# Local attention layers on one core: masks in the scores' row tiles, and a new order of the stages on all engines

## The chip, the cores and the metric

The program runs on one core of one Trainium2 chip. The metric is the device time of one execution in microseconds. Three executions took 3747.89, 3753.0 and 3758.61 us; the median is 3753.0 us.

## The reference

Inputs are x and a context of shape (32, 128, 128): 32 batch elements, 128 tokens, width 128. The model is a gated cross-attention, a stack of six local-attention layers with an MLP each, a second gated cross-attention and an int8 product. The change is in the six local layers:

```
for i in range(DEPTH):                                   # 6
    x = attn_layer(shift_tokens(x), Wqkv[i], ...) + x    # 16 heads of 64, window 32
    x = ffn_layer(shift_tokens(x), ...) + x              # layer norm, 128 -> 2 x 341, a * gelu(gate), -> 128
...
    q = l2norm(q) * qs;  k = l2norm(k) * ksc             # then rotary tables on both
    mask = (it < jb) | (it > jb + w) | (jb == -1)        # a window sees itself and the window before
    sim = where(mask, -max, einsum(q, k) * QK_SCALE)     # (windows of 32 queries) x (64 keys)
    attn = softmax(sim, -1)
    out = einsum(attn, v)                                # then out @ Wo
```

## The kernel before

**Units and groups.** A unit is one batch element in one layer: 6 x 32 = 192 units. A group is four units (512 tokens), and the output projection, the MLP and its layer norm run once a group. Everything is fp32, except the masks, which are bf16.

**The software pipeline.** Each engine (TensorE `pe`, ScalarE `act`, VectorE `dve`, GpSimd `pool`, and SyncE `sp` for the DMAs) has a loop over steps at the end of its function in `local_layers`. In step s it calls its stages for unit s, s-1, s-2 and so on, in the order in which they are written there. No scheduler moves anything: each engine works through its own list in order, and semaphores hold a stage until what it reads is made and what it overwrites is read. The number in `scores(step - 2)` is the lag of that stage.

**A unit's way.** `project` makes q, k and v (lines L697; two products of 512 columns each). q and k share one pair of PSUM banks, QK_PAIR: ScalarE squares what stands there (`square`, L874), VectorE multiplies it with the cosine and sine tables (`products`, L1012 and L1013), and only then is the pair free for the next projection. VectorE sums the squares (L1020) and clamps them (L1028), ScalarE makes the reciprocal norms (L883, L885), GpSimd adds the rotary halves (`rotate`, L1121) and multiplies with the norms (`normalise`, L1129). TensorE turns q and k (`transpose_qk`, L707), ScalarE copies them out (L892). `scores` first writes the masks into the scores' banks (L717, a product of the identity with the mask table) and adds the products of q and k (L726), in array tiles of 64 rows and 32 columns. VectorE takes the maxima and subtracts them (L1033, L1041), ScalarE exponentiates (L899), VectorE sums rows (L1049, L1051), GpSimd normalises (L1113), TensorE turns the weights (L738), ScalarE copies them (L906), and TensorE mixes the values (`mix`, L763) in tiles of 64x64. ScalarE copies the mix (L913). v goes through ScalarE's copy (L867) and four DMAs that place it again in other partitions (`place_v`).

**Once a group.** `project_out` (L777), the mean (L786), the variance (L794), three upper products of the MLP in tiles of 128, 128 and 85 hidden channels (`mlp_up`, L804), their GELU on ScalarE (`mlp_gelu`, L965) and product on VectorE (`mlp_hidden`, L1075), and `mlp_down` (L815). The steps repeat with period four: one step has no group work, one has the mean and the MLP products, one the variance, one the output projection.

**PSUM.** Pair 0 of banks is the scores', pair 1 is QK_PAIR. All other stages take pairs 2 and 3 in turn, in the order of the table ALTERNATING, which follows TensorE's order. A stage therefore waits until the stage two places before it has been read out.

Of the kernel before, what the change touches and what calls it, by code (L numbers as in the profile page):

```python
# [47 lines left out]
CONSTS = 2 * P + NEAR + 4 * HD + 4  # L48
# [62 lines left out]
def build(nc, dram):  # L111
    stack = ExitStack()
    with stack:
# [14 lines left out]
        tables = consts[:, 2 * P + NEAR:CONSTS - 4].rearrange("p (k s d) -> p k s d", k=4, s=2)  # L128
        ident_bf = sb("ident_bf", [P, P], BF16)
        mask_band = sb("mask_band", [P, IT, NEAR], BF16)  # L130
        mask_past = sb("mask_past", [P, GB, P], BF16)
# [8 lines left out]
        MASKS = 2 + GB  # L140
# [404 lines left out]
        def local_layers(phase):  # L545
            here = ExitStack()
            with here:
# [37 lines left out]
                for n in ("squared", "producted", "summed", "rotations", "normalised", "turned", "copied"))  # L585
# [14 lines left out]
            ALTERNATING = (("mix", 4, 1), ("v", 2, 1), ("up0", 10, GB), ("mean", 6, GB), ("up1", 10, GB), ("variance", 7, GB),  # L600
                           ("up2", 10, GB), ("probs", 3, 1), ("out", 4, GB), ("k", 1, 1), ("down", 10, GB), ("q", 1, 1))
# [76 lines left out]
            def pe(pe):  # L678
# [33 lines left out]
                def scores(u):  # L712
# [97 lines left out]
                def mlp_down(g):  # L810
# [3 lines left out]
                    for t, (o, n) in enumerate(FTILES):  # L814
                        mm = pe.matmul(pairs[i][:, 0:GT], w_2[0:n, t, :], gelu[0:n, t, :], start=t == 0,  # L815
                                       stop=t == len(FTILES) - 1)
                    mm.then_inc(down_made, 1)

                for step in range(UNITS + LAST):
                    project(step, 0)  # L820
                    mix(step - 4)
                    project(step - 2, 2)
                    mlp_up(step - 10, 0)
                    scores(step - 2)
                    project(step, 1)
                    mlp_mean(step - 6)
                    mlp_up(step - 10, 1)
                    mlp_variance(step - 7)
                    mlp_up(step - 10, 2)
                    transpose_probs(step - 3)  # L830
                    project_out(step - 4)
                    transpose_qk(step - 1, 1)
                    mlp_down(step - 10)
                    transpose_qk(step - 1, 0)
                phase_end(pe)

            def act(act):
# [121 lines left out]
                def mlp_gelu(g, t):  # L959
                    o, n = FTILES[t]  # L960
                    tables_at["exp"] = False
                    act.wait_ge(up_made, 3 * g + t + 1)
# [5 lines left out]
                for step in range(-1, UNITS + LAST):  # L968
                    square(step, 0)
                    prepare(step + 1)  # L970
                    mlp_affine(step - 10)
                    mlp_root(step - 8)
                    mlp_square(step - 7)
                    copy_mix(step - 4)
                    reciprocal_norms(step - 1)
                    mlp_shift(step - 5)
                    mlp_gelu(step - 10, 0)
                    copy_v(step - 2)
                    square(step, 1)
                    mlp_log(step - 7)  # L980
                    mlp_gelu(step - 10, 1)
                    mlp_gelu(step - 10, 2)
                    copy_probs(step - 3)
                    copy_qk(step - 1, 1)
                    exponentials(step - 2)
                    copy_qk(step - 1, 0)
                phase_end(act)

            def dve(dve):
# [82 lines left out]
                def mlp_hidden(g, t):  # L1072
                    o, n = FTILES[t]
                    dve.wait_ge(gelu_made, 3 * g + t + 1)
# [11 lines left out]
                for step in range(UNITS + LAST):  # L1086
                    if step < UNITS and step % NB == 0:
                        start_layer(step // NB)
                    row_sums(step - 3)
                    products(step, 0)  # L1090
# [3 lines left out]
                    mlp_hidden(step - 10, 1)  # L1094
# [772 lines left out]
```

## Time and profile before

| | |
|---|---|
| median of three executions | 3753.0 us |
| profiled execution | 3750.37 us |
| its span, first to last instruction | 3748.6 us |
| granted TensorE clock, mean | 0.985 |
| TensorE busy | 3555.1 us, 95% |
| VectorE busy | 2719.1 us, 73% |
| ScalarE busy | 2447.7 us, 65% |
| GpSimd busy | 2283.3 us, 61% |

Busy time counts matmuls with modelled ends, which overlap; where the text needs the cost of a stage, it is the distance from its first start to the next stage's first start. An fp32 matmul stands in the trace as two records. In rows of a timeline the last bracket is the idle time before the row and what ended it.

### The profile page before, as it was taken

To read this page: it belongs to the slowest core of one execution; us is meant where nothing else is said; L and a number is where in the kernel's file an instruction comes from. 1 tells how busy PE (TensorE), PEld (TensorE's weight loads), DVE (VectorE), ACT (ScalarE), POOL (GpSimd) and SP (SyncE) were. 2 spreads that over 40 slices of the span, in tenths; PEclk is the share of its full clock that TensorE was granted. 3 is DMA by queue.
4 is the path that set the end of the run, shared out by engine and by line. 5 is a ranking of instruction groups with operands and counts; after the bars stand their busy time and mean duration, and the time that the engine had idled before them with its cause. 6 is when DMAs were issued, how large, how long until landed. Compare 5 with 4: busy or idle time off the path is not lost.

```text
span 3748.6 us, 131464 instructions
## 1 busy us (share of the span) xinstructions
PE 3555.1 (95%) x57538; PEld 2099.7 (56%) x57538; DVE 2719.1 (73%) x3104; ACT 2447.7 (65%) x4388; POOL 2283.3 (61%) x1216
## 2 busy tenths in 40 slices
PE   8979999999999999999999999999999999997996
PEld 4535555555555555555555555555555555553554
DVE  6858777777777777777777777777777777763787
ACT  6856666666666666666666666666666666664985
POOL 1227666666666666666666666666666666652666
PEclk9989999999999999999999999999999999998998
DMA  2001111111111111111111111111112111120000
GB/s 86 2 1 42 36 36 32 46 47 42 36 31 36 53 40 38 36 36 47 45 40 36 35 32 53 42 41 36 30 37 58 32 40 36 36 58 2 2 10 15
DMA packets 90943, 134.71 MB, mean 36 GB/s; under 512 B 23686, under 2 KB 37380, under 8 KB 89988
## 3 DMA queue, kind: packets, MB, share of 16 engines
q1 hardware_dynamic: 90372, 126.29, 13.0%
q8 instruction: 456, 7.47, 0.9%
q14 instruction: 115, 0.94, 0.1%
HBM read 23.48 MB, written 2.10 MB: 7 GB/s over the span
## 4 chain that ended last, share of the span: by engine, by line
PE 81%; ACT 6%; DVE 6%; issue 5%; POOL 1%; DMA 0%; SPq 0%; POOLq 0%; DVEq 0%; ACTq 0%
PE psum L697 29%; PE psum L777 8%; PE psum L763 8%; PE psum L726 7%; PE psum L804 7%; PE psum L707 6%; PE psum L815 3%; PE psum L738 2%; PE psum L717 2%; DVE f_times_sin L1013 2%; ACT f_squares L874 2%; ACT f_probsT L906 1%; ACT x_expo L1446 1%; PE psum L786 1%; PE psum L794 1%
## 5 line engine op out<-in xcount | busy, mean ns | idle before, releaser
L1121 POOL TENSOR_TENSOR f_rotated<-f_times_cos,f_times_sin 128x1024 f32<-128x1024 f32 x384 | 906.4, 2361 | 527.3 <-DVE f_times_sin L1013 527.3
L697 PE MATMUL psum<-w_qkv,f_xs 128*128 128x512 f32 x2304 | 1135.7, 616 | 40.2 <-DVE f_times_sin L1013 35.4
L874 ACT ACTIVATE f_squares<-psum 128x1024 f32<-128x1024 f32 x384 | 393.8, 1026 | 530.1 <-PE psum L697 530.1
L1129 POOL TENSOR_TENSOR f_rotated<-f_rotated,f_rnorm 128x1024 f32<-128x1024 f32 x384 | 722.3, 1902 | 26.5 <-ACT f_rnorm L885 26.5
L1113 POOL TENSOR_TENSOR f_probs<-f_probs,f_rowsum 128x1024 f32<-128x1024 f32 x192 | 365.2, 1902 | 537.6 <-DVE f_rowsum L1051 537.6
L892 ACT COPY f_qkT<-psum 128x1024 f32<-128x1024 f32 x384 | 388.4, 1011 | 351.5 <-PE psum L707 346.6
L697 PEld LDWEIGHTS psum<-w_qkv,f_xs 128*128 128x128 f32 x2304 | 393.7, 191 | 362.0 <-issue 284.6
L1012 DVE TENSOR_TENSOR f_times_cos<-psum,rot 128x1024 f32<-128x1024 f32 x384 | 460.4, 1199 | 88.7 <-ACT f_squares L874 86.5
L1013 DVE TENSOR_TENSOR f_times_sin<-psum,rot 128x1024 f32<-128x1024 f32 x384 | 465.6, 1212 | 0.0
L1020 DVE TENSOR_REDUCE f_sumsq<-f_squares 128x16 f32<-128x1024 f32 x384 | 451.8, 1208 | 0.0
L707 PE MATMUL psum<-consts,f_rotated 128*128 128x128 f32 x3072 | 408.1, 278 | 44.8 <-DVE f_gelu L1075 27.7
L707 PEld LDWEIGHTS psum<-consts,f_rotated 128*128 128x128 f32 x3072 | 340.1, 141 | 145.1 <-issue 50.5
L1033 DVE TENSOR_REDUCE f_negmax<-psum 128x16 f32<-128x1024 f32 x192 | 234.8, 1223 | 217.9 <-PE psum L726 217.7
L763 PEld LDWEIGHTS psum<-f_probsT,f_v 64*64 64x64 f32 x6144 | 262.1, 135 | 145.8 <-issue 145.5
L777 PE MATMUL psum<-f_outT,w_o 128*128 128x512 f32 x768 | 339.1, 595 | 1.2 <-ACT f_outT L913 1.2
L763 PE MATMUL psum<-f_probsT,f_v 64*64 64x64 f32 (+1 forms) x6144 | 309.3, 228 | 1.3 <-issue 1.1
L763 PE MATMUL psum<-f_probsT,f_v_moved 64*64 64x32 f32 (+1 forms) x12288 | 306.7, 217 | 0.0
L726 PEld LDWEIGHTS psum<-f_qkT 64*32 64x32 f32 x24576 | 250.1, 105 | 82.9 <-issue 82.8
L763 PEld LDWEIGHTS psum<-f_probsT,f_v_moved 64*64 64x64 f32 x12288 | 285.4, 135 | 0.0
L726 PE MATMUL psum<-f_qkT 64*32 64x64 f32 (+1 forms) x24576 | 281.7, 219 | 1.0 <-issue 1.0
L804 PE MATMUL psum<-f_xn,w 128*128 128x512 f32 (+1 forms) x576 | 265.9, 598 | 7.4 <-ACT f_xn L955 6.7
L738 PEld LDWEIGHTS psum<-consts,f_probs 128*128 128x128 f32 x1536 | 175.9, 141 | 111.2 <-issue 78.4
(179 smaller groups left out, 5237.3 us busy)
## 6 DMA issues: line engine op xcount, KB each, us to landing
f_v_moved<-f_v SPq DMA_DIRECT2D x768, 128.0 KB, 2.5
w_qkv<-in_l_wqkv SPq DMA_DIRECT2D x18, 512.0 KB, 3.7
w_o<-in_l_wo SPq DMA_DIRECT2D x6, 512.0 KB, 4.4
w_qkv<-in_ctxT SPq DMA_DIRECT2D x1, 2048.0 KB, 8.3
out<-x_f_result SPq DMA_DIRECT2D x8, 256.0 KB, 2.2
w<-in_l_w SPq DMA_DIRECT2D x6, 341.0 KB
xres<-in_xT SPq DMA_DIRECT2D x1, 1536.0 KB, 8.8
x_ctx<-in_ctxT SPq DMA_DIRECT2D x1, 1536.0 KB, 12.0
```

What stands on the lines that cost most here:

```text
L697: mm = pe.matmul(pairs[i][:, j * BANK:(j + 1) * BANK], xs[g % 2][:, u % GB, :], w_qkv[:, part * INNER + j * BANK:part * INNER + (j + 1) * ...
L707: tr = pe.transpose(pairs[i][:, t * S:(t + 1) * S], rotated[u % 2][:, part, 2 * t:2 * t + 2, :].rearrange("p h d -> p (h d)"), ident)
L726: mm = pe.matmul(pairs[SCORE_PAIR][these, at:at + near.stop - near.start], qkT[u % 2][rows, 0, t, these], qkT[u % 2][rows, 1, t, near], st ...
L763: mm = pe.matmul(pairs[i][cols, at + queries.start:at + queries.stop], values, probsT[u % 2][rows, j, queries], start=True, stop=True, til ...
L777: mm = pe.matmul(pairs[i][:, 0:GT], w_o[:, t, :], outT[:, t, :], start=t == 0, stop=t == IT - 1)
L804: mm = pe.matmul(pairs[i][0:n, a * BANK:a * BANK + GT], w_1[:, a * FF + o:a * FF + o + n], xn[:, :], start=True, stop=True)
L874: act.activation(squares[part][:, :], pairs[QK_PAIR], ACT.Square).then_inc(squared[part], 1)
L1012: dve.tensor_tensor(halves(times_cos[part][:, :]), halves(pair), table(0), ALU.mult)
L1013: dve.tensor_tensor(halves(times_sin[part][:, :]), halves(pair)[:, ::-1], table(1), ALU.mult).then_inc(producted[part], 1)
L1020: dve.tensor_reduce(sumsq[u % 2][:, part * H:(part + 1) * H], squares[part][:, :].rearrange("p (s h d) -> p h s d", s=2, h=H), axis=XY, op ...
L1121: pool.tensor_tensor(rotated[u % 2][:, part].rearrange("p h (s d) -> p s h d", s=2), halves(times_cos[part][:, :]), halves(times_sin[part] ...
L1129: pool.tensor_tensor(rt, rt, rnorm[u % 2][:, part * H:(part + 1) * H].unsqueeze(2).broadcast_to([P, H, HD]), ALU.mult).then_inc(normalised ...
```

## The change

Two things change, and both are in the local layers.

**Masks.** Before, each of the two mask products multiplies a 128x128 identity with the mask table for all 128 query rows. Now the table holds the 64 kinds of query rows that differ (the first window's 32, and the later windows' 32), twice, once for each half of the partitions, and a new matrix `mask_pick` picks for each of the 128 queries its kind. So a mask product contracts over 64 rows, and the two products, one for each bank, stand in the upper and the lower 64 rows of the array. `mask_pick` is one more block of 128 columns in the constants and one more copy to bf16 on VectorE at the start.

**Order.** The stages stand in another order on TensorE, ScalarE, VectorE and GpSimd; v is projected one unit after q and k rather than two; the three upper products are made in the order 2, 1, 0; some stages that ended a step on one engine now begin the next one with a lag one higher (the sum of squares of k, the clamp), and some group stages of ScalarE and GpSimd move to another lag.

```
-                        pe.matmul(pairs[SCORE_PAIR][:, j * BANK:(j + 1) * BANK], ident_bf[:, :],
-                                  mask_band[:, :, :].rearrange("p g n -> p (g n)"), start=True, stop=False)
+                        rows = slice(HD * j, HD * j + HD)
+                        pe.matmul(pairs[SCORE_PAIR][:, j * BANK:(j + 1) * BANK], mask_pick[rows, :],
+                                  mask_band[rows, :, :].rearrange("p g n -> p (g n)"), start=True, stop=False,
+                                  tile_position=(rows.start, 0))
...
-                    banks.fill(pe, i, (hidden_made, 3 * g + t + 1))
+                    banks.fill(pe, i, (hidden_made, 3 * (g + 1) - t))
...
                 for step in range(UNITS + LAST):          # TensorE
+                    mlp_up(step - 10, 2)
                     project(step, 0)
+                    mlp_up(step - 10, 1)
+                    mlp_up(step - 10, 0)
+                    project(step - 1, 2)
+                    scores(step - 2)
                     mix(step - 4)
-                    project(step - 2, 2)
-                    mlp_up(step - 10, 0)
-                    scores(step - 2)
+                    mlp_mean(step - 6)
                     project(step, 1)
-                    mlp_mean(step - 6)
-                    mlp_up(step - 10, 1)
                     mlp_variance(step - 7)
-                    mlp_up(step - 10, 2)
                     transpose_probs(step - 3)
                     project_out(step - 4)
-                    transpose_qk(step - 1, 1)
                     mlp_down(step - 10)
                     transpose_qk(step - 1, 0)
+                    transpose_qk(step - 1, 1)
...
+                for step in range(-2, UNITS + LAST):      # ScalarE, whole
+                    mlp_gelu(step - 10, 2)
+                    mlp_shift(step - 6)
+                    mlp_gelu(step - 10, 1)
                     square(step, 0)
+                    mlp_affine(step - 9)
+                    mlp_gelu(step - 10, 0)
+                    copy_v(step - 1)
+                    reciprocal_norms(step - 1)
                     mlp_root(step - 8)
+                    prepare(step + 2)
                     mlp_square(step - 7)
                     copy_mix(step - 4)
                     square(step, 1)
                     mlp_log(step - 7)
                     copy_probs(step - 3)
+                    copy_qk(step - 1, 0)
+                    exponentials(step - 2)
                     copy_qk(step - 1, 1)
-                    exponentials(step - 2)
-                    copy_qk(step - 1, 0)
...
                     products(step, 0)                     # VectorE, in part
-                    mlp_hidden(step - 10, 0)
+                    sum_squares(step, 0)
+                    row_maxima(step - 2)
                     mlp_centre(step - 6)
-                    row_maxima(step - 2)
...
-                    sum_squares(step, 1)
-                    clamp_norms(step)
...
                     normalise_probs(step - 3)             # GpSimd, whole
+                    normalise(step - 1, 0)
                     normalise(step - 1, 1)
-                    normalise(step - 1, 0)
                     rotate(step, 0)
                     rotate(step, 1)
+                    mlp_scale(step - 8)
```

On TensorE, before, around a step with the mean and the MLP products. L697 is a projection, L738 turns the weights, L707 turns q and k, L804 are the upper products, L815 the down product:

```order
6410 L697 MATMUL psum<-w_qkv,f_xs 128x512 x2
6411 L786 MATMUL psum<-f_mlp_xs,mean_mat 128x512
6412 L804 MATMUL psum<-f_xn,w 128x512 x2
6413 L804 MATMUL psum<-f_xn,w 85x512 x2
6414 L738 MATMUL psum<-consts,f_probs 128x128 x8
6415 L707 MATMUL psum<-consts,f_rotated 128x128 x8
6416 L815 MATMUL psum<-f_gelu,w 128x512 x3
6417 L707 MATMUL psum<-consts,f_rotated 128x128 x8
```

The same engine in the change, from the k projection of the step without group work to the masks of the step with the MLP products (L698, L741, L708, L807 and L719 are L697, L738, L707, L804 and L717 of before):

```order
6221 L698 MATMUL psum<-w_qkv,f_xs 128x512 x2
6222 L741 MATMUL psum<-consts,f_probs 128x128 x8
6223 L708 MATMUL psum<-consts,f_rotated 128x128 x16
6224 L807 MATMUL psum<-f_xn,w 85x512 x2
6225 L698 MATMUL psum<-w_qkv,f_xs 128x512 x2
6226 L807 MATMUL psum<-f_xn,w 128x512 x4
6227 L698 MATMUL psum<-w_qkv,f_xs 128x512 x2
6228 L719 MATMUL psum<-mask_band,mask_pick 128x512 x2
```

All three upper products have moved ahead of the masks, the first of them to between the turn of k and the next q projection; before, two stood right ahead of the turns and one behind the value projection. And later in that step, in the change, ending with the first projections of the next step:

```order
6277 L789 MATMUL psum<-f_mlp_xs,mean_mat 128x512
6278 L698 MATMUL psum<-w_qkv,f_xs 128x512 x2
6279 L741 MATMUL psum<-consts,f_probs 128x128 x8
6280 L818 MATMUL psum<-f_gelu,w 128x512 x3
6281 L708 MATMUL psum<-consts,f_rotated 128x128 x16
6282 L698 MATMUL psum<-w_qkv,f_xs 128x512 x4
```

The down product now stands ahead of both turns, and the q and the v projection stand together (x4). The mix rows, which stood between them, follow the scores.

## Rows read from the trace of the kernel before

**Rows 1.** The page, part 1: busy us (share of the span) x instructions, by engine.
```profile
PE 3555.1 (95%) x57538; PEld 2099.7 (56%) x57538; DVE 2719.1 (73%) x3104; ACT 2447.7 (65%) x4388; POOL 2283.3 (61%) x1216
```
**Rows 2.** Timeline of TensorE (start, length, operation, [idle before]), the output projections.
```profile
996.04 4.46 PE L777 MATMUL psum<-f_outT,w_o 128*128 128x512 f32 x10
...
1061.10 7.03 PE L777 MATMUL psum<-f_outT,w_o 128*128 128x512 f32 x16
```
**Rows 3.** Timeline of TensorE, step without group work, to the next mix.
```profile
1009.95 0.59 PE L717 MATMUL psum<-mask_band,ident_bf 128*128 128x512 bf16 x2
1010.48 1.46 PE L726 MATMUL psum<-f_qkT 64*32 64x32 f32 x128
1011.87 1.98 PE L697 MATMUL psum<-w_qkv,f_xs 128*128 128x512 f32 x4
1013.69 1.04 PE L738 MATMUL psum<-consts,f_probs 128*128 128x128 f32 x8
1014.56 1.04 PE L707 MATMUL psum<-consts,f_rotated 128*128 128x128 f32 x8
1015.87 1.09 PE L707 MATMUL psum<-consts,f_rotated 128*128 128x128 f32 x8 [0.27 <-ACT f_probsT L906]
1017.36 1.98 PE L697 MATMUL psum<-w_qkv,f_xs 128*128 128x512 f32 x4 [0.39 <-DVE f_times_sin L1013]
1019.27 0.27 PE L763 MATMUL psum<-f_probsT,f_v 64*64 64x64 f32 x1
```
**Rows 4.** Timeline of TensorE, from the mean to the down product.
```profile
1028.08 1.02 PE L786 MATMUL psum<-f_mlp_xs,mean_mat 128*128 128x512 f32 x2
1028.94 3.60 PE L804 MATMUL psum<-f_xn,w 128*128 128x512 f32 x8
1032.38 1.09 PE L738 MATMUL psum<-consts,f_probs 128*128 128x128 f32 x8
1034.09 1.10 PE L707 MATMUL psum<-consts,f_rotated 128*128 128x128 f32 x8 [0.62 <-DVE f_gelu L1075]
1035.03 2.74 PE L815 MATMUL psum<-f_gelu,w 128*128 128x512 f32 x6
```
**Rows 5.** Timeline of TensorE in the second cross-attention, from 128*128 to 128*32 tiles.
```profile
3500.62 1.02 PE L1290 MATMUL psum<-y,x_wq 128*128 128x512 f32 x2
3501.58 1.08 PE L1327 MATMUL psum<-x_probsT,x_vpad 128*32 128x128 f32 x32
```
**Rows 6.** Timeline of TensorE in the first cross-attention: masks behind 32*128 tiles.
```profile
66.21 0.61 PE L294 MATMUL psum<-mask_past,ident_bf 128*128 128x512 bf16 x2
66.75 1.16 PE L301 MATMUL psum<-x_queries,x_keys 32*128 32x128 f32 x16
```
**Rows 7.** Timeline of TensorE in the second cross-attention: two 32-row tiles.
```profile
3472.13 1.13 PE L1303 MATMUL psum<-x_keys,x_queries 32*128 32x512 f32 x4
3473.19 0.98 PE L1313 MATMUL psum<-consts,x_expo 128*128 128x128 f32 x7
```
**Rows 8.** Timelines of ScalarE and VectorE around the stages of rows 3 and 4.
```profile
1013.89 1.02 ACT L874 ACTIVATE f_squares<-psum 128x1024 f32<-128x1024 f32 x1 [2.05 <-PE psum L697]
1014.81 1.01 ACT L906 COPY f_probsT<-psum 128x1024 f32<-128x1024 f32 x1
1015.70 1.03 ACT L892 COPY f_qkT<-psum 128x1024 f32<-128x1024 f32 x1
...
1022.42 1.28 ACT L965 ACT_TABLE_LOAD   x1
1024.54 0.69 ACT L965 ACTIVATE f_gelu<-psum,b 128x512 f32<-128x512 f32 x1 [0.84 <-PE psum L804]
...
1016.09 1.21 DVE L1013 TENSOR_TENSOR f_times_sin<-psum,rot 128x1024 f32<-128x1024 f32 x1
...
1025.26 0.75 DVE L1075 SCALAR_TENSOR_TENSOR f_gelu<-psum,b,f_gelu 128x512 f32<-128x512 f32 x1 [1.78 <-ACT f_gelu L965]
```
**Rows 9.** Timeline of GpSimd, the two products with the norms.
```profile
1009.75 3.77 POOL L1129 TENSOR_TENSOR f_rotated<-f_rotated,f_rnorm 128x1024 f32<-128x1024 f32 x2
```

More of the change, by code:

```diff
@@ L47 @@
 HALFV = INNER // 2
-CONSTS = 2 * P + NEAR + 4 * HD + 4
+CONSTS = 3 * P + NEAR + 4 * HD + 4
 VSTEP = P + XD
@@ L139, in build @@
         phase_over = sem("phase_over")
-        MASKS = 2 + GB
+        MASKS = 3 + GB
         def group(t, g):
@@ L599, in local_layers @@
             LAST = 11
-            ALTERNATING = (("mix", 4, 1), ("v", 2, 1), ("up0", 10, GB), ("mean", 6, GB), ("up1", 10, GB), ("variance", 7, GB),
-                           ("up2", 10, GB), ("probs", 3, 1), ("out", 4, GB), ("k", 1, 1), ("down", 10, GB), ("q", 1, 1))
+            ALTERNATING = (("up2", 10, GB), ("up1", 10, GB), ("up0", 10, GB), ("v", 1, 1), ("mix", 4, 1), ("mean", 6, GB),
+                           ("variance", 7, GB), ("probs", 3, 1), ("out", 4, GB), ("down", 10, GB), ("q", 1, 1), ("k", 1, 1))
             pair_of, turn = {}, 0
@@ L813, in mlp_down @@
                     pe.wait_ge(hidden_made, 3 * g + 3)
-                    for t, (o, n) in enumerate(FTILES):
-                        mm = pe.matmul(pairs[i][:, 0:GT], w_2[0:n, t, :], gelu[0:n, t, :], start=t == 0,
-                                       stop=t == len(FTILES) - 1)
+                    for t, (o, n) in reversed(list(enumerate(FTILES))):
+                        mm = pe.matmul(pairs[i][:, 0:GT], w_2[0:n, t, :], gelu[0:n, t, :], start=t == len(FTILES) - 1,
+                                       stop=t == 0)
                     mm.then_inc(down_made, 1)
                 for step in range(UNITS + LAST):
+                    mlp_up(step - 10, 2)
                     project(step, 0)
+                    mlp_up(step - 10, 1)
+                    mlp_up(step - 10, 0)
+                    project(step - 1, 2)
+                    scores(step - 2)
                     mix(step - 4)
-                    project(step - 2, 2)
-                    mlp_up(step - 10, 0)
-                    scores(step - 2)
+                    mlp_mean(step - 6)
                     project(step, 1)
-                    mlp_mean(step - 6)
-                    mlp_up(step - 10, 1)
                     mlp_variance(step - 7)
-                    mlp_up(step - 10, 2)
                     transpose_probs(step - 3)
                     project_out(step - 4)
-                    transpose_qk(step - 1, 1)
                     mlp_down(step - 10)
                     transpose_qk(step - 1, 0)
+                    transpose_qk(step - 1, 1)
                 phase_end(pe)
@@ L1088, in dve @@
                         start_layer(step // NB)
+                    sum_squares(step - 1, 1)
+                    clamp_norms(step - 1)
                     row_sums(step - 3)
+                    mlp_hidden(step - 10, 2)
+                    mlp_hidden(step - 10, 1)
+                    mlp_hidden(step - 10, 0)
                     products(step, 0)
-                    mlp_hidden(step - 10, 0)
+                    sum_squares(step, 0)
+                    row_maxima(step - 2)
                     mlp_centre(step - 6)
-                    row_maxima(step - 2)
-                    mlp_hidden(step - 10, 1)
-                    mlp_hidden(step - 10, 2)
                     lower(step - 2)
@@ L1098, in dve @@
                     add_out(step - 4)
-                    sum_squares(step, 0)
                     add_down(step - 10)
-                    sum_squares(step, 1)
-                    clamp_norms(step)
                 phase_end(dve)
@@ L1807, in shape_constants @@
     parts = (np.arange(P)[:, None] % XPAD // XD == np.arange(4)[None, :])
-    return np.concatenate([np.eye(P), band, past] + both + [parts], axis=1).astype(np.float32)
+    kinds = np.concatenate([band[0:2 * WIN]] * 2)
+    row = np.arange(P)
+    kind = np.where(row < WIN, row, WIN + row % WIN)
+    pick = np.arange(P)[:, None] % (2 * WIN) == kind[None, :]
+    return np.concatenate([np.eye(P), kinds, past, pick] + both + [parts], axis=1).astype(np.float32)
 def halves_first(w):
```

18 lines of the change are left out of this document (5 added, 13 removed).

## The prediction

> **What bounds the kernel now.** The page comes first: TensorE is busy 95% of the span [rows 1]. So TensorE's own stream sets the time, and a change is worth what it takes out of that stream: work, changes of tile size, or waits. The local layers repeat every four units. In TensorE's timeline the output projection L777 starts at 996.04 and again at 1061.10 us [rows 2]: a group of four units takes 65.06 us. There are 48 groups (6 layers of 32 elements), some 3,120 of the 3,750 us.
>
> The timeline in order of time then shows where the 65.06 us go. The number to read is the distance from one row's start to the next one's, since a row's own length includes the pipeline's tail. In a step without group work [rows 3]: masks 0.53, scores 1.39, k projection L697 1.82, turn of the weights 0.87, turn of q, a pause, turn of k, a pause, next q projection. I read three pauses off the starts:
>
> - The turn of k starts 1.31 after the turn of q (1014.56 to 1015.87) where eight transposes need 0.87: 0.44 lost. The row names the copy of the turned weights on ScalarE.
> - Eight transposes after a wait take 0.94 (1034.09 to 1035.03, [rows 4]), so k's end at 1016.80; the q projection starts at 1017.36: 0.56 lost, and the row names VectorE's product with the sine table, which reads the PSUM pair that q and k share. The q projection then takes 1.91 to the mix where 1.72 of work (twice the 0.86 of two matmul records, 1028.08 to 1028.94) and 0.09 for the change of tile size make 1.81: 0.10 more, a weight load that a waiting engine could not fetch early.
> - In the step with the MLP's upper products [rows 4], the turn of q starts 1.71 after the turn of the weights: 0.84 lost, named to VectorE's L1075 on f_gelu, which frees the PSUM pair that the third upper product used; and 0.07 more for the first load.
>
> **The change part by part, on TensorE.** All sums are per unit (192) or per group (48).
>
> Masks. Masks to scores, 0.53, holds two bf16 products over all 128 rows (2 x 0.22) and 0.09 for the change from the full array to the scores' tiles. What a change of size costs is also seen where only the columns change: L1290 (two records, full array) to L1327 (128*32) is 0.96, and two such records without a change are 0.86 (L786 to L804), so 0.10. The two new products sit in different halves of the rows and write different banks. Nearest row: L1303, two 32-row tiles with 512 columns, writing two banks. Four records in 1.06 [rows 7]; one after another four fp32 records are 1.72, side by side two passes are 0.86 plus the change 0.09 and an open first load 0.10 = 1.05. So pairs in different row tiles run together, and I take 0.22 for both masks instead of 0.43: -0.21 a unit. Bound from the other side: not together, 0.
>
> First loads. After a change back to the full array, the first fp32 matmul is 0.10 late (k's projection 1.82 [rows 3] against 1.72; the value projection stands behind small tiles as well, so twice a unit). Afterwards the value projection stands right behind q or the upper products, in the same layout: 1.72. -0.10 a unit. In its place the masks now come right after a change. What a bf16 load costs there: L294 follows 32-row tiles and takes 0.54 to its successor [rows 6], L717 without such a change 0.53 [rows 3]: 0.01. The Trainium skill ("TensorE: Matmul & The Clock Gate", The mechanism and LDWEIGHTS) says that a load overlaps running matmuls only in another row group and takes columns / 1.2 GHz, an estimated 0.107 here; by that the masks' load lies open and the total is 18 us higher. The row of this case has 0.01, and I go by it.
>
> Changes of tile size. Before, four a unit: into the mix, out, into the scores, out. Afterwards also four: into 64x128, to 64x32, to 64x64, out. No row shows a change between two small sizes with the same 64 rows. Bounds: 0, or the 0.09 that every recorded change costs. The nearest row is L1290 to L1327, where the rows stay 128 and only the columns change, at the full 0.10 [rows 5]. So I take 0.09 and no gain; the other end is 2 x 0.09 x 192 = 35 us less. The Trainium skill ("TensorEngine Tiling (Array Packing)", Key Properties) says that a change of the tiling mode drains the array while a change of tile doesn't. That rule speaks against a gain from putting scores and mix together; read loosely, with 64 rows as one mode, it would give the 35 us. The column row agrees with the strict reading.
>
> Waits. I walked the new order on all four engines with durations from the rows. Take the k projection's start in a plain step as 0 (before: 1011.87).
> ScalarE squares k at 2.02, copies the turned weights at 2.94 to 3.95, and k's turn can start at 4.00 [rows 3, 8]. This chain is untouched: 0.44 stays.
> K's turn ends at 4.93. VectorE's sine product starts at 4.22, takes 1.21 [rows 8] and lets a q projection start at 5.49. Before, q stood there and waited. Now the first upper product (85 columns wide, 1.72) does: it needs the pair of the turned q, which ScalarE now copies first, 3.83 to 4.86, free at 4.90. So it starts at 4.93, and q at 6.65, without a wait: -0.56 and its reload -0.10.
> The other upper products run at 8.37 and 10.09, the value projection at 11.80. It needs the pair of the second upper product: done at 10.26 (8.37 + 1.72 + the 0.17 by which a record outlasts the next start), GELU 0.69, VectorE's product 0.75, free near 11.80 [rows 8]. No wait, but only just. ScalarE's table load of 1.28 falls at about 6.7, ahead of the first GELU and hidden behind the q projection.
> The last upper product's VectorE step is done near 13.5, the down product asks for it at about 20: the wait of 0.84 and its 0.07 are gone. The down product now stands ahead of both turns, and k's turn then waits for VectorE to add it into y; I find 0.10, with 0.06 of reload.
> The waits in the steps with the variance and the output projection have unchanged chains and cancel. Together: -0.66 -0.91 +0.16 = -1.41 a group.
>
> Other engines. VectorE gets one copy of 128x128 at the start, beside the loads: 0.2 us at most. The constants are 64 KB longer in one load. Neither counts. The sum of squares of k and the clamp move behind the next step's start, so the normalisation of a unit starts later: in my walk GpSimd is done with k's 7.8 us into the step that turns it, and TensorE comes for it at 9.4; before the same pair of 1.9 us multiplications was done at 1013.52 for turns that started at 1014.56 [rows 3, 9].
>
> **Sum.** 4 x (-0.21 - 0.10) - 1.41 = -2.65 a group, 62.4 instead of 65.06. Over 47.5 groups (the first ones are not full): -126 us. The profiled execution took 3750.4 us (span 3748.6), so 3624; the median of the runs is 2.6 above it: 3627.
>
> **The rivals.**
> 1. Changes between the small sizes are free, or the mix's first loads hide behind the scores: 35 us more, 3592. For it: the row halves stay the same. Against: the column row.
> 2. The masks don't run side by side in 64x128 tiles (+0.21 x 192 = 40), or their first load lies open like an fp32 one (+0.10 x 192 = 19): 3646 to 3667. For it: no 64*128 row exists. Against: L1303.
> 3. The waits only move. The walk has two places with under 0.05 us to spare (the upper product after the copy of q, the value projection after the second VectorE product). If both steps lose all again, only masks and loads are left: 60 us, 3693. For it: every engine is in order, and ScalarE's table load sits in that step. Against: a late copy by 0.2 costs 0.2 a group, 10 us, not all.
> 4. Slower: normalisation. GpSimd's two products of 1.9 us start when ScalarE has made the norms; ScalarE now does that behind the copy of v, and VectorE's part behind the next step's start. To spare: 1.5 us. If the norms come later than that, TensorE waits before the turn of k in every unit, and from 1.5 + 126/192 = 2.2 us late the gain is used up. Two more VectorE operations of 1.2 us in that chain make 2.4: (2.4 - 2.2) x 192 = 38 us over before, 3791. I find no such pair in the order, and the products of the next q stand behind the clamp.
> 5. No effect, TensorE's stream held by something that the trace hides: 3750.
>
> **How the numbers follow.** Forecast 62% (own range 3608 to 3645: the walk's small margins, 10 us each way, and the masks' load), rival 1 15%, rival 2 10%, rival 3 7%, rival 4 4%, rival 5 2%. The range 3590 to 3672 holds the first three. 0.3% is 11 us, about what a measurement tells from no change; faster by more than that are the first four, 94%.
>
> **What would show it.** In the new timeline: masks to scores 0.32 (right) or 0.53 (rival 2); scores to mix about 1.39 with the first mix row 0.09 late (rival 1: 1.30); value projection 1.72; first upper product right behind k's turn, q after it without an idle remark; no idle of 0.6 named to L1075 before a turn; groups of 62.4. A row of the turn waiting for GpSimd's f_rotated would mean rival 4. The forecast fails if the period of the groups is above 63.2 or below 61.8.

## The result and the profile after

The change made the kernel slower: 3938.7 us (median of four executions) against 3752.4 before, ratio 1.050, 95% interval 1.047 to 1.053. The forecast was 3627, faster.

The page of the changed kernel, part 1 (busy us, share, instructions), and its chain by engine:

```profile
span 3939.5 us, 131465 instructions
...
PE 3587.2 (91%) x57538; PEld 2138.5 (54%) x57538; DVE 2838.7 (72%) x3105; ACT 2444.7 (62%) x4388; POOL 2284.6 (58%) x1216
...
PE 80%; issue 10%; ACT 5%; DVE 3%; POOL 1%; DMA 0%; SPq 0%; POOLq 0%; DVEq 0%; ACTq 0%
```

In the chain of before, "issue" had 5%.

Read this against [rows 1]. The instructions of TensorE are the same in number, and no other engine is near its limit. But TensorE is idle for 3939.5 - 3587.2 = 352 us where it was 3748.6 - 3555.1 = 194. Its busy time grew by 32 us too, and the mean granted clock fell from 0.985 to 0.971.

What the forecast said of single places is there, but for one. TensorE's timeline of the changed kernel, from the turn of k in the step with the upper products to the mix (the window's edge cuts the first row; rows of one or two instructions within the mix are left out):

```profile
1548.74 0.82 PE L708 MATMUL psum<-consts,f_rotated 128*128 128x128 f32 x6
1549.39 1.93 PE L807 MATMUL psum<-f_xn,w 128*85 128x512 f32 x4
1551.17 1.88 PE L698 MATMUL psum<-w_qkv,f_xs 128*128 128x512 f32 x4
1552.88 3.60 PE L807 MATMUL psum<-f_xn,w 128*128 128x512 f32 x8
1556.33 1.98 PE L698 MATMUL psum<-w_qkv,f_xs 128*128 128x512 f32 x4
1558.24 0.39 PE L719 MATMUL psum<-mask_band,mask_pick 64*128 64x512 bf16 x2
1558.56 1.46 PE L729 MATMUL psum<-f_qkT 64*32 64x32 f32 x128
1559.95 0.27 PE L766 MATMUL psum<-f_probsT,f_v 64*64 64x64 f32 x1
...
1562.62 0.21 PE L766 MATMUL psum<-f_probsT,f_v_moved 64*64 64x64 f32 x1 [1.30 <-issue]
```

Masks to scores 0.32, scores to mix 1.39, the first upper product right behind the turn of k, then q 1.78 later with no idle remark: as written. The value projection is the exception. It was to take 1.72 and takes 1.91 (1556.33 to 1558.24): 0.10 is the change to the masks' tiles, and 0.10 an open first load, because that load has to wait for VectorE to free the PSUM pair, once a group (PEld are the weight loads):

```profile
PEld psum L698 <- DVE f_gelu L1078: 30.4, 45, 0.7
```

The last line of the timeline is the new thing. In the middle of the mix TensorE stands still for 1.30 us, and the row names no engine, no semaphore and no DMA, only "issue": it waited for nothing that the profile shows. TensorE's waits, of before and then of after (whom it waited for: us in total, times, longest):

```profile
PE psum L697 <- DVE f_times_sin L1013: 35.4, 57, 3.5
PE psum L707 <- DVE f_gelu L1075: 27.7, 45, 0.6
PE psum L707 <- ACT f_probsT L906: 13.6, 50, 0.3
...
PE psum L763 <- issue: 1.1, 1, 1.1
```

```profile
PE psum L766 <- issue: 188.4, 124, 2.7
PE psum L729 <- issue: 19.8, 34, 1.0
...
PE psum L708 <- ACT f_probsT L909: 13.3, 50, 0.3
PE psum L698 <- DVE f_times_sin L1016: 12.3, 10, 3.5
```

The two waits that the forecast wanted gone are gone (35.4 to 12.3; the one on f_gelu ahead of a turn has no row any more), and the third stayed as said. In their place stand 208 us of pauses inside the blocks of mix and scores.

**Where they fall.** TensorE's timeline of the changed kernel around one unit in which the scores and the projection behind the mix are hit (most rows of the mix are left out):

```profile
1539.20 1.15 PE L729 MATMUL psum<-f_qkT 64*32 64x32 f32 x98
1541.16 0.45 PE L729 MATMUL psum<-f_qkT 64*32 64x32 f32 x30 [0.81 <-issue]
...
1541.67 0.35 PE L766 MATMUL psum<-f_probsT,f_v_moved 64*64 64x64 f32 x10
...
1543.07 0.70 PE L698 MATMUL psum<-w_qkv,f_xs 128*128 128x512 f32 x1
1545.00 1.45 PE L698 MATMUL psum<-w_qkv,f_xs 128*128 128x512 f32 x3 [1.23 <-issue]
```

Count the instructions from one pause to the next: 30 products of scores, 96 of the mix and 1 of the projection, each with its weight load, and the load of the next. That is 255, and a wait for a semaphore in between is an instruction too. The DMA part of the page has a queue for instructions:

```profile
q8 instruction: 456, 7.47, 0.8%
```

456 packets with 7.47 MB, 16 KB each. TensorE's 57,538 matmuls, 57,538 loads, 1,656 waits for semaphores and 4 drains are 116,736 instructions, which is 456 x 256 exactly: one packet of this queue is 256 instructions of TensorE. Number them in the order of the trace, and 157 of the 158 pauses in scores and mix (207 us) lie at the same place modulo 256, within two instructions; without the waits for semaphores in the count they scatter over all places.

The trace also has the time of every packet, and it ties the two together. The pause at the k-th of these borders ends 1.1 to 1.6 us after the end of the k-th packet, in all 157 cases, and in no run here is a border crossed earlier than 1.08 us after the end of its packet. A packet takes 0.9 to 1.9 us, and the nearest two in any run start 3.20 us apart.

In before the queue moved the same 456 packets, and TensorE had two such pauses, of 0.5 us each, in the scores (its one idle remark in a mix, 1.1 us, stands once in every run, at another place modulo 256). What changed is how fast the instructions are used up: the 256 of a block of scores take 1.39 us and the 192 of a mix 1.53, and now they stand back to back, 448 instructions in 2.9 us, where before a value projection (16 instructions in 1.82) stood between them [rows 3].

**The clock.** Mean values of the changed kernel in four stretches (us from the start: length, busy us and instructions of each engine, then the granted clock of TensorE, the DMA share, GB/s), and its timeline there:

```profile
1430.00:1434.00 4.00, 4.00 (x74) 1.82 (x76) 3.21 (x5) 3.31 (x4) 1.95 (x2) 1.00 0.00 0
1434.00:1438.10 4.10, 2.43 (x181) 2.23 (x165) 4.07 (x4) 2.33 (x6) 3.61 (x3) 0.99 0.42 100
1438.10:1441.50 3.40, 3.40 (x18) 1.78 (x15) 0.30 (x1) 1.01 (x1) 2.63 (x2) 0.50 0.14 39
1441.50:1445.00 3.50, 3.45 (x21) 2.23 (x20) 1.99 (x2) 2.89 (x4) 0.00 (x0) 1.00 0.00 0
```

```profile
1429.56 3.60 PE L698 MATMUL psum<-w_qkv,f_xs 128*128 128x512 f32 x8
...
1433.41 1.46 PE L729 MATMUL psum<-f_qkT 64*32 64x32 f32 x128
...
1437.93 0.38 PE L766 MATMUL psum<-f_probsT,f_v_moved 64*64 64x32 f32 x8 [1.67 <-issue]
...
1438.44 3.47 PE L698 MATMUL psum<-w_qkv,f_xs 128*128 128x512 f32 x4
```

After a pause of 1.67 us the granted clock is 0.50 (1.2 in place of 2.4 GHz) for 3.4 us, and a projection that lasts 1.98 [rows 3] lasts 3.47. From 270 to 3400 us the changed kernel is at half clock in 36 stretches (123 us), before in 3 (17 us). All but one of the 36 begin within 2 us of the end of a pause of 1.5 us or more, but 42 further pauses of that length, up to 2.7 us, have no such stretch behind them.

### The profile page after: what moved, and what is told of

It reads as the page before. It is cut to its first block, busy times and chain, and to the rows that moved or that the text cites. A ratio compares the mean times of both kernels' runs of the same rounds, so it can differ in the third digit from the quotient of the medians.

```text
span 3939.5 us, 131465 instructions
## 1 busy us (share of the span) xinstructions
PE 3587.2 (91%) x57538; PEld 2138.5 (54%) x57538; DVE 2838.7 (72%) x3105; ACT 2444.7 (62%) x4388; POOL 2284.6 (58%) x1216
## 3 DMA queue, kind: packets, MB, share of 16 engines
q8 instruction: 456, 7.47, 0.8%
## 4 chain that ended last, share of the span: by engine, by line
PE 80%; issue 10%; ACT 5%; DVE 3%; POOL 1%; DMA 0%; SPq 0%; POOLq 0%; DVEq 0%; ACTq 0%
PE psum L698 27%; PE psum L766 8%; PE psum L780 8%; PE psum L708 7%; PE psum L729 7%; PE psum L807 6%; PE psum L741 3%; PE psum L818 3%; ACT f_probsT L909 2%; PE psum L719 2%; PE psum L789 2%; ACT x_expo L1449 1%; PE psum L797 1%; PE psum L1306 1%; PE psum L1316 1%
## 5 line engine op out<-in xcount | busy, mean ns | idle before, releaser
L698 PE MATMUL psum<-w_qkv,f_xs 128*128 128x512 f32 x2304 | 1131.5, 625 | 20.7 <-DVE f_times_sin L1016 12.3
L1132 POOL TENSOR_TENSOR f_rotated<-f_rotated,f_rnorm 128x1024 f32<-128x1024 f32 x384 | 722.3, 1902 | 299.7 <-ACT f_rnorm L888 299.7
L698 PEld LDWEIGHTS psum<-w_qkv,f_xs 128*128 128x128 f32 x2304 | 427.1, 197 | 484.8 <-issue 429.7
L895 ACT COPY f_qkT<-psum 128x1024 f32<-128x1024 f32 x384 | 389.3, 1014 | 427.3 <-PE psum L708 425.6
L916 ACT COPY f_outT<-psum 128x1024 f32<-128x1024 f32 x192 | 194.4, 1012 | 439.1 <-PE psum L766 434.2
L1023 DVE TENSOR_REDUCE f_sumsq<-f_squares 128x16 f32<-128x1024 f32 x384 | 464.4, 1209 | 0.0
L766 PE MATMUL psum<-f_probsT,f_v_moved 64*64 64x32 f32 (+1 forms) x12288 | 337.8, 218 | 124.7 <-issue 124.5
L708 PE MATMUL psum<-consts,f_rotated 128*128 128x128 f32 x3072 | 407.1, 278 | 18.9 <-ACT f_probsT L909 13.3
L708 PEld LDWEIGHTS psum<-consts,f_rotated 128*128 128x128 f32 x3072 | 340.2, 141 | 117.7 <-issue 51.3
L766 PE MATMUL psum<-f_probsT,f_v 64*64 64x32 f32 (+1 forms) x6144 | 335.5, 228 | 63.9 <-issue 63.9
L766 PEld LDWEIGHTS psum<-f_probsT,f_v_moved 64*64 64x64 f32 x12288 | 302.7, 135 | 125.2 <-issue 124.6
L766 PEld LDWEIGHTS psum<-f_probsT,f_v 64*64 64x64 f32 x6144 | 277.8, 135 | 95.2 <-issue 77.8
L1052 DVE TENSOR_REDUCE f_rowsum<-f_probs 128x16 f32<-128x1024 f32 x192 | 232.8, 1213 | 58.6 <-ACT f_probs L902 58.6
L807 PE MATMUL psum<-f_xn,w 128*128 128x512 f32 (+1 forms) x576 | 267.1, 600 | 4.5 <-ACT f_xn L958 3.7
```

Of the source, the lines that this page charges most:

```text
L698: mm = pe.matmul(pairs[i][:, j * BANK:(j + 1) * BANK], xs[g % 2][:, u % GB, :], w_qkv[:, part * INNER + j * BANK:part * INNER + (j + 1) * ...
L708: tr = pe.transpose(pairs[i][:, t * S:(t + 1) * S], rotated[u % 2][:, part, 2 * t:2 * t + 2, :].rearrange("p h d -> p (h d)"), ident)
L766: mm = pe.matmul(pairs[i][cols, at + queries.start:at + queries.stop], values, probsT[u % 2][rows, j, queries], start=True, stop=True, til ...
L807: mm = pe.matmul(pairs[i][0:n, a * BANK:a * BANK + GT], w_1[:, a * FF + o:a * FF + o + n], xn[:, :], start=True, stop=True)
L1023: dve.tensor_reduce(sumsq[u % 2][:, part * H:(part + 1) * H], squares[part][:, :].rearrange("p (s h d) -> p h s d", s=2, h=H), axis=XY, op ...
L1132: pool.tensor_tensor(rt, rt, rnorm[u % 2][:, part * H:(part + 1) * H].unsqueeze(2).broadcast_to([P, H, HD]), ALU.mult).then_inc(normalised ...
```

## The experiments

Theory A says that TensorE's instructions come in packets of 256 and that two borders can't be crossed less than about 3.5 us apart, so two dense blocks mustn't stand together. In that form it is too strong, as the traces show: single pairs of borders are crossed 1.2 to 2.5 us apart, 12 times in before and 34 times in the changed kernel (270 to 3350 us), when the second packet was already there. It is the packets that keep the distance. Rival M puts the loss down to the masks in 64-row tiles, rival O to semaphores that the new order makes late.

**The masks alone,** in the order of before:

```
+                        rows = slice(HD * j, HD * j + HD)
-                        pe.matmul(..., ident_bf[:, :], mask_band[:, :, :]...
+                        pe.matmul(..., mask_pick[rows, :], mask_band[rows, :, :]..., tile_position=(rows.start, 0))
```

> The order of stages of before, with the new masks alone. Theory A (instruction supply): TensorE's records (loads and products) arrive in packets of 256, and no two boundaries between packets can be crossed less than about 3.5 us apart; in before's order the 192 records of a mix and the 256 of a block of scores have a value projection of 1.8 us between them or on each side, so no stalls appear: 3753 - 192 x 0.21 = 3713, or about 3730 if half of the gain turns into waits for ScalarE; no pauses inside blocks of scores or mix. Rival M (the products in 64-row tiles are themselves what stalls, because the scores now follow the masks without a change of tile): most of the 186 us that the change lost is there: 3900 or more.

Measured: 3723.6 us, ratio 0.993 (0.992 to 0.995), 29 us faster, where 23 to 40 were expected. TensorE's pauses in scores and mix are those of before (2.4 us in all, 2.1 before). Rival M is out.

**The new order with the masks of before:**

> The new order of stages on all engines, with the masks of before. Theory A: scores and mix still stand back to back (448 records of TensorE in about 3 us), so the pauses of 0.5 to 2.7 us inside both blocks stay, some 150 of them, and with the dearer masks the time is 3940 to 3980. Rival M: without masks in row tiles nothing stalls, and the order saves the waits that the forecast counted: about 3670. Rival O (the order makes semaphores late, and the pauses are waits): 3940 to 3980 too, so this run doesn't tell A from O.

Measured: 3942.6 us, ratio 1.051 (1.048 to 1.053), as theory A and rival O had it. The loss belongs to the order, whole (L764 is the mix, L727 the scores):

```profile
PE psum L764 <- issue: 179.7, 120, 2.5
PE psum L727 <- issue: 11.9, 24, 0.9
```

**The order of before with one stage moved,** so that mix, masks and scores touch. Its table of PSUM pairs follows; nothing else changes.

```
                     mix(step - 4)
-                    project(step - 2, 2)
                     mlp_up(step - 10, 0)
                     scores(step - 2)
+                    project(step - 2, 2)
```

> The kernel before with one line moved and nothing else: the value projection goes behind the block of scores, so that mix, masks and scores stand back to back (192 and 260 records in 3.4 us). Its consumer, ScalarE's copy of the values, stands far enough behind to meet no new wait. Theory A: pauses appear inside mix and scores in a kernel that had none, at every 256th record: 50 to 200 us more, 3800 to 3950, and stretches of half clock with them. Rivals M and O: 3753 within 10 us, since no wait for a semaphore and no mask changes.

Measured: 3869.1 us, ratio 1.031 (1.030 to 1.033), 116 us slower. No mask changed, yet the pauses are there (L726 are the scores), 84 of them, and they name no engine:

```profile
PE psum L726 <- issue: 84.1, 84, 2.4
PE psum L804 <- ACT f_xn L955: 23.7, 48, 3.7
```

The second line is a wait that my expectation had ruled out: the first upper product now stands right behind the mix and meets ScalarE's f_xn once a group, 17 us more than before (6.7 in 2 waits). (A row L717 <- issue of 23.2 us, some 0.16 us each time, is no idle time: the trace lacks the record of one of the two mask products.) That is all of this run that rival O could claim. The 84 pauses lie at the borders of packets, each ends 1.2 to 1.6 us behind its packet's end, so this run decides for A, and rivals M and O, which had 3753 here, are out. The granted clock stayed at 0.983, with 4 slow stretches, fewer than I had counted on. So 84 of the 116 us are pauses in the scores, 17 the new wait, and 8 are clock (0.985 - 0.983 of 3870); the rest carries no name of its own.

**The supply measured by itself.** In before, the masks and scores of the first unit are made 17 times:

```
+                    for again in range(17 if u == 0 else 1):
                         for j in range(2):
                             pe.matmul(pairs[SCORE_PAIR][:, j * BANK:(j + 1) * BANK], ident_bf[:, :], ...
```

> The kernel before, with the masks and scores of the very first unit made 17 times in a row into the same banks (the result is the same). 16 more blocks of 260 records, 0.53 + 1.39 = 1.92 us each by the rows of before. If TensorE's speed is what sets them: 31 us, 3784. Theory A: each 256 records take at least about 3.5 us, with a pause at every 256th record in the trace: 16.25 x 3.5 = 57 us, some 3810, and inside that stretch the packets of the instruction queue follow one another without a gap between them of more than 3 us.

Measured: 3803.1 us in one execution, 50 more than the median of before, where 31 was expected of TensorE's own speed and 57 of theory A; the timeline says it better (L718 masks, L727 scores):

```profile
278.46 1.08 PE L727 MATMUL psum<-f_qkT 64*32 64x32 f32 x88
280.65 0.66 PE L727 MATMUL psum<-f_qkT 64*32 64x64 f32 x40 [1.10 <-issue]
281.24 0.60 PE L718 MATMUL psum<-mask_band,ident_bf 128*128 128x512 bf16 x2
281.77 1.07 PE L727 MATMUL psum<-f_qkT 64*32 64x32 f32 x86
284.10 0.68 PE L727 MATMUL psum<-f_qkT 64*32 64x64 f32 x42 [1.26 <-issue]
284.71 0.61 PE L718 MATMUL psum<-mask_band,ident_bf 128*128 128x512 bf16 x2
285.25 1.02 PE L727 MATMUL psum<-f_qkT 64*32 64x32 f32 x84
287.56 0.69 PE L727 MATMUL psum<-f_qkT 64*32 64x64 f32 x44 [1.29 <-issue]
```

A block has 130 products, and the pause comes after 88, 86, 84 of the scores: 40 + 2 + 86 = 128 products with their loads from pause to pause, so it slides back by two in each block. The first three pauses end at 280.65, 284.10 and 287.56, 3.45 us apart (3.45 to 3.73 over all 16 in this stretch), and blocks that would take 1.92 take 3.47. From 278.46 to 334 us the DMA part has

```profile
q1 hardware_dynamic: 316, 0.52, 3.7%
q8 instruction: 15, 0.25, 1.7%
```

15 packets in 55.5 us, 3.7 us each, with the DMA engines otherwise nearly idle: it isn't the traffic of the four DMAs that place v that slows them.

**Half of the mix.** The changed kernel without the products of t = 2 and 3, half of the mixing left out:

```
-                    for t in range(IT // 2):
+                    for t in range(IT // 4):
```

> The changed kernel with half of the mixing left out (products for the first half of the heads' pairs only, 96 records of TensorE in 0.77 us in place of 192 in 1.53), so its output lacks that half; no wait and no place in the order changes. The work left out is worth 192 x 0.77 = 148 us, so a theory in which the pauses have nothing to do with the number of instructions gives 3939 - 148 = 3791. Theory A: 352 records stand close together, not 448, so fewer pairs of boundaries fall within 3.5 us, and the pauses shrink by about half, 100 us or more beyond the work: 3620 to 3710.

Measured: 3618.0 us, 2 below the expected range. 321 us went, of which 148 were the work. The queue has 384 packets, 72 fewer, and 192 x 96 / 256 is 72. The pauses fell from 208 to 85 us and the granted clock rose to 0.983:

```profile
PE psum L766 <- issue: 69.0, 54, 2.0
PE psum L729 <- issue: 15.6, 28, 1.1
```

**Two blocks apart, first try.** The changed kernel with the scores ahead of the value projection, so that this stands between scores and mix:

```
-                    project(step - 1, 2)
                     scores(step - 2)
+                    project(step - 1, 2)
                     mix(step - 4)
```

> The changed kernel with one line moved: the block of scores goes ahead of the value projection, so that this projection (1.7 us, 16 records) stands between scores and mix. Theory A: the two dense blocks are apart again, the pauses inside them go to under 20 us in sum, the granted clock is back at about 0.985, and the time falls from 3939 to 3690 to 3760; not to 3627, since ScalarE's copy of the values and what stands behind it come about 1.9 us later. Rival O: the pauses are ScalarE's or VectorE's lateness, which this move only makes worse: 3940 or more. Rival M: 3939, since the masks are as they were.

Measured: 3827.5 us, ratio 1.021 (1.019 to 1.022): 111 us better than the change, but not the 3690 to 3760 expected. Pauses fell to 49 us, most of them still in the scores. The rest is a new wait, for the copies of q and k on ScalarE ahead of the masks (L719):

```profile
PE psum L719 <- ACT f_qkT L895: 45.2, 138, 2.0
PE psum L729 <- issue: 44.7, 30, 2.3
```

I put the rest of the loss down to ScalarE's queue: it waited 604.7 us at the copy of v (121.2 in the change) ahead of the inverse norms, for which GpSimd waited 719.6 (299.7). The next run moves that copy behind the norms:

```
-                    copy_v(step - 1)
                     reciprocal_norms(step - 1)
+                    copy_v(step - 1)
```

> The run with scores, value projection, mix in that order, which stayed at 3827, with one more line moved: ScalarE makes the inverse norms ahead of its copy of the values. There ScalarE waited 605 us at that copy (121 in the changed kernel) and GpSimd 720 us for the inverse norms (300). If this wait in ScalarE's queue is what kept that run above the kernel before: GpSimd's wait falls to about 300 us and the time to 3720 to 3780. If it is the pauses that were left in the scores (45 us) and the clock, the time stays within 20 us of 3827.

Measured: 3777.7 us, ratio 1.008 (1.006 to 1.009), 50 us better and at the edge of what was expected. GpSimd's wait fell to 154.7 us. TensorE's waits before turns and upper products that the queue had caused (15.2 us for f_spread, 8.6 for f_rotated, 8.2 for f_gelu) went to 0.5 and 0.8 us or have no row any more, and its pauses fell from 49 to 38 us, so the queue was the cause for the larger part of the 50. But TensorE still waits 44.0 us for L895 and 34.0 in pauses in the scores.

The traces say where these two come from. In the changed kernel the masks start 1.46 to 1.61 us after ScalarE's copy of k has ended, in the three steps of four without upper products. Taking the value projection from in front of them brings them forward by more than that, so TensorE now waits right ahead of the masks (138 times, 0.33 us on average). Of the 30 units with a pause in the scores, 22 have such a wait of 0.27 to 0.35 us: there the packet that ends the pause starts 0.9 to 1.3 us after the masks, and the pause lasts 1.55 to 2.31 us. In 7 of the 8 others the packet starts 0.5 to 0.8 us before the masks, and the pause lasts 0.41 us at most; the eighth, 1.84 us without a wait, is an exception. So a single block of scores, with a value projection behind it, stalls by itself where TensorE had to wait just ahead of it. I read this as a request for the next packet that goes out late because TensorE stands at the wait; no run varies that wait alone.

**Two blocks apart, second try.** The mix goes ahead of the value projection, as in before, and ScalarE copies v behind its copy of the mix. All else is the new order:

```
+                    mix(step - 4)                # TensorE; the PSUM pair of mix likewise ahead of v
                     project(step - 1, 2)
                     scores(step - 2)
-                    mix(step - 4)
...
-                    copy_v(step - 1)             # ScalarE
                     reciprocal_norms(step - 1)
...
                     copy_mix(step - 4)
+                    copy_v(step - 1)
```

> The changed kernel with two lines moved: the mix goes ahead of the value projection (so mix, projection, masks and scores in that order, the two dense blocks 1.8 us apart as in before), and ScalarE copies the values behind its copy of the mix, so that the copy's wait doesn't stand ahead of the inverse norms, which is what the run with the value projection behind the scores lost most by. All the rest of the new order stays. Theory A: hardly any pauses (under 30 us), granted clock about 0.985, and the savings that the forecast counted are there, less 0.1 to 0.2 us a unit for the first loads and one more change of tile size: 3753 - 126 + 35 = 3660, range 3630 to 3760. Rival O (the new order itself makes something late): 3800 or more.

Measured: 3667.6 us, ratio 0.977 (0.976 to 0.979), 86 us faster than before and 271 faster than the change. TensorE is busy 96% of the span (3524.8 us), and the pauses in scores and mix are gone:

```profile
PE psum L729 <- issue: 2.9, 4, 1.2
PE psum L766 <- issue: 1.1, 1, 1.1
```

Its timeline, two output projections and a unit's blocks:

```profile
1488.84 7.03 PE L780 MATMUL psum<-f_outT,w_o 128*128 128x512 f32 x16
...
1533.18 1.98 PE L698 MATMUL psum<-w_qkv,f_xs 128*128 128x512 f32 x4
1535.10 0.39 PE L719 MATMUL psum<-mask_band,mask_pick 64*128 64x512 bf16 x2
1535.42 1.46 PE L729 MATMUL psum<-f_qkT 64*32 64x32 f32 x128
...
1552.23 7.03 PE L780 MATMUL psum<-f_outT,w_o 128*128 128x512 f32 x16
```

A group takes 63.39 us where it took 65.06 [rows 2], the same in nearly all groups (the changed kernel's groups have 69.0 in the middle, and none is without a pause).

**The same with the masks of before,** to price the masks:

> The faster version (mix, value projection, masks, scores, with ScalarE's copy of the values behind its copy of the mix) with the masks of before in place of those in 64-row tiles. It prices the new masks in an order in which TensorE hardly waits: the forecast's 0.21 us a unit gives 3668 + 40 = 3708. If part of the masks' gain is again lost in a wait for another engine, as in the run with the masks alone (29 us of 40), it is 3690 to 3700; if the masks in row tiles bring nothing here, 3668.

Measured: 3682.1 us, ratio 0.982 (0.980 to 0.983). The masks are worth 14 us by the two medians, 17 by the two ratios to before, not 40. The timeline above says why: the value projection takes 1.92 (1533.18 to 1535.10) ahead of masks in 64-row tiles, 1.82 ahead of masks over all rows [rows 3], because the array changes its tiles at the masks and again at the scores. 0.21 - 0.10 = 0.11, times 192 is 21 us, and the groups agree: 63.82 us with the masks of before, 63.39 with the new ones, 0.43 for four units. My expectations for this run and for the masks alone had left out the second change.

## Why the prediction was wrong

**Bound now.** Right: TensorE's stream sets the time, also in every run here.

**Masks: -0.21 a unit.** Right at its place (0.53 to 0.32), and 0.22 for both masks, so they run side by side. But masks in 64-row tiles bring one more change of tiles, 0.10, in every order, so by themselves they are worth 0.11 a unit. The prediction's count of four changes before and four afterwards set this one off against the one that scores and mix save by standing together, so its sum holds.

**First loads: -0.10.** Right in three steps of four: q and v together take 1433.41 - 1429.56 - 0.32 = 3.53 (before 1.91 behind a wait or 1.81 for q [rows 3], and 1.82 for v), which is twice 1.72 and 0.09 for the change of tiles, so no bf16 load lies open behind it. In the step with the upper products the load of v's weights lies open, 0.10 once a group, some 5 us in all. The walk had this place ("No wait, but only just"), and rival 3 its kind.

**Waits.** Right in kind: of the 35.4 us for f_times_sin 12.3 are left, the wait for f_gelu ahead of a turn went, the one for f_probsT stayed. Rival 4 (late normalisation) didn't come: TensorE waited 3.0 us in all for f_rotated, in three places.

**Changes of tile size: "no gain" from putting scores and mix together.** This is the step that failed. It asked what the neighbourhood is worth to the array and took 0 for the worse end. It has a cost that none of my terms held: 448 instructions in 2.9 us, from a supply whose packets of 256 start 3.2 us apart at the least. The missing term is 208 us of pauses that carry a name, and the half clock after some of the longer ones: (0.985 - 0.971) x 3939 is some 55 us.

Against the forecast of 3627 the kernel is 312 us late. The faster version, which differs only in where mix and ScalarE's copy of v stand, splits that. 271 us lie between the two kernels: in the profiled executions TensorE is idle 352 us against 143, which is 209 more and nearly all pauses, and busy 3587.2 against 3524.8, which is 62 more, where the half clock shows. The other 41 lie between the faster version and the forecast, and 35 of them were expected there, for one more change of tile size and one more first load a unit. So the rest of the forecast's sum was right to some 6 us as a whole, and the missing term is nearly the whole miss.

The range failed for the same reason: none of the five rivals was about how instructions reach an engine, and the only slower one, with 4 in 100, was another.

**Could it have been seen?** The rows were there. Scores are 128 products with 128 loads in 1.39 us, 5 ns an instruction, and the instruction queue's 456 packets stand in before's page. What before didn't show is the price, since it had only two such pauses, of 0.5 us each. The Trainium skill ("Runtime: NRT & Kernel Launch", Instruction fetch mechanics) says that instructions are refilled in blocks of 256 while the engine executes, and that the cost of a border is mostly hidden because the engine issues more slowly than the refill works. The block of 256 agrees with this trace (the packets and the places of the pauses). That the border is hidden agrees with before, with 1 us of pauses at 456 borders, and not with the changed kernel, where small tiles are issued at 5 to 8 ns and a border costs up to 2.7 us.

## What to carry to other kernels

Before two blocks of many short matmuls are put side by side, count instructions, loads included, against time: here 256 in less than 3.5 us, twice in a row, stalls TensorE, while one such block with a few long matmuls on either side costs next to nothing, unless TensorE has just waited for another engine right ahead of it. A long projection between dense blocks isn't only work, it is the time in which instructions arrive; moving it away cost 208 us of pauses, where the two waits that the new order removed had been worth some 50. And an idle remark that names no engine, in the middle of a block whose operands are all there, is worth counting instructions for, from one such row to the next.

## What the hardware showed that I had not expected

- The instruction supply of TensorE: one packet of 16 KB for 256 instructions, waits for semaphores included, and when TensorE wants them at once one packet in 3.45 to 3.73 us. TensorE goes on 1.1 to 1.6 us after a packet's end. A single block of 256 in 1.39 us mostly passes unhindered, but behind a wait for ScalarE it stalled by up to 2.3 us.
- The clock can fall behind a pause of the supply: after 1.67 us of standing still the granted clock was 0.50 for 3.4 us. Among the repeated scores, with 16 pauses of 1.1 to 1.6 us one after another, no stretch of half clock stands, and the run with 84 pauses in the scores has 4. What in a pause decides it, I leave open.
- Each change of tile costs 0.09 to 0.10 us, also a second one right behind the first: full array to 64x128 tiles (1.92 for 1.82) and 64x128 to 64x32 (0.32, 0.22 of it the two products side by side).
